# Attention layer of a four-layer graph kernel: scores from split halves, the mask on GpSimd, the normalisation shared with ScalarE

## The chip, the cores and the metric

The kernel runs on one core of a Trainium2 chip. The time is the device time of one execution, in microseconds (us). Five engines work side by side, each through its own queue in order: TensorE (PE in the profile), VectorE (DVE), ScalarE (ACT), GpSimd (POOL), and SyncE (SP), which here only starts transfers. They meet at semaphores: an instruction waits until a counter has reached a value. GpSimd works on SBUF alone; the other three reach PSUM too, into which TensorE writes.

## What is computed

Input `x` has 64 batches of 256 nodes with 128 features, `adj` is a 256x256 mask of zeros and ones. Four layers follow one another, each of the form `x = layernorm(x + layer(x))`. The change is in layer 0, the attention:

```python
def _L0_gnn_ref(x, A_shape, q, k, v):
    Q = x @ q
    K = x @ k
    A = jnp.einsum('bnd,bmd->bnm', Q, K)
    A = A / jnp.sqrt(jnp.float32(input_dimension))
    A = jnp.tanh(A / 8.0) * 8.0
    A = jnp.exp(A) * A_shape
    A = A / jnp.sum(A, axis=-1, keepdims=True)
    out = A @ x @ v
    return out

x = _layernorm(x + _L0_gnn_ref(x, adj, L0_gnn_q, L0_gnn_k, L0_gnn_v), axis=-1)
```

Layer 1 is five steps of a gated recurrence over `adj`, layer 2 a graph convolution up to the third power of `adj`, layer 3 a message layer. They are not touched.

## The kernel before

**Tiling.** Two batches make a group of 512 nodes, four tiles of 128 nodes; there are 32 groups. All five engines run the attention in slots, one group entering in each slot: `s` is the slot, and a step with a lag of L works in slot s on group s - L. The slots 0 to 7 and the last ones are written out, those between are a loop of four slots. Nothing schedules this: the order in which an engine's `slot` function names its steps is the order of its queue. In the profile's lines the functions `tensor`, `scalar`, `vector` and `gpsimd` of `attention_layer` are at L331 to L407, L410 to L438, L440 to L499 and L280 to L330.

**One group's way.** TensorE transposes `x` (L355) into a PSUM bank, ScalarE copies it to `x_t` (L417). TensorE forms the qk product `p` of it (L374; `qk` is q times k transposed, made once) and `x v` (L380), which ScalarE copies to `p_t` (L431) and `xv` (L434). A slot later TensorE forms the scores (L365), and ScalarE takes their tanh (L422) and exp (L426). VectorE multiplies by the mask (L449, 128x1024 numbers), TensorE sums over the nodes (L346; a column of ones in `xv` gives the denominator), VectorE takes the reciprocal (L454), scales and adds `x` (L457), takes the statistics (L462, `BN_STATS` in the order, `BATCH_NORM_STATS2` in the profile), combines them with six small instructions of 4 to 12 columns (L132 to L140, `combine_stats`), GpSimd raises the variance to the power -1/2 (L329, `ALU.pow`), and VectorE normalises (L475). SyncE stores the result.

**Types.** The matrix products of the attention are plain float32. The later layers split each operand instead into a `_hi` part of type float32r and a `_lo` part, the rest of it, and make three float32r products: hi by hi, lo by hi, hi by lo. The split takes a cast (ScalarE or GpSimd) and a subtraction (VectorE or GpSimd).

**What sets the order around the change.** TensorE's slot is: sum over the nodes of group s-3, transposes of s, scores of s-1, qk product and `x v` of s. ScalarE's is: `x_t` of s, tanh and exp of s-1, `p_t` and `xv` of s. VectorE's is: mask of s-2; reciprocal, scaling and statistics of s-3; normalisation of s-4; combining of s-3. GpSimd has one power a slot; before its first slot it prepares the weights of the later layers. `weave` lets the slots of the gated layer (layer 1) begin inside the last slots of the attention, at the numbers given to it, on each engine by itself:

```python
both = weave(attention["gpsimd"](pool), gated["gpsimd"](pool), [30, 31, 32, 33])
both = weave(attention["tensor"](pe), gated["tensor"](pe), [31, 32, 33, 34])
both = weave(attention["vector"](dve), gated["vector"](dve), [31.5, 32.5, 33.5, 34.5])
```

In those slots the gated layer's steps stand between the attention's: transposes L651, products with `adj` L663 and L665, gate products L676 to L708 on TensorE, `hn_lo` L758, `m_lo` L767 and `rh` L773 on VectorE, `rh_lo` L626, `h_hi` L630 and `h_lo` L632 on GpSimd.

Of the kernel before, what the change touches and what calls it, by code (L numbers as in the profile page):

```python
# [35 lines left out]
def adj_resnorm_d4_kernel(nc, t, out):  # L36
# [14 lines left out]
    with ExitStack() as top:  # L51
# [33 lines left out]
        with ExitStack() as ctx_gated:  # L85
# [4 lines left out]
            with ExitStack() as ctx_conv:  # L90
# [35 lines left out]
def combine_stats(dve, stats, moments, parts, var_eps, parts_done, terms_done, var_done, n):  # L126
# [11 lines left out]
    dve.tensor_scalar(moments[:, :, 1], moments[:, :, 1], 0.5, None, ALU.mult).then_inc(terms_done, 1)  # L138
# [4 lines left out]
def attention_layer(nc, t, psum, env, ctx):  # L143

    KC, N, D, GB, TILES, COLS, GROUPS = (env[k] for k in ("KC", "N", "D", "GB", "TILES", "COLS", "GROUPS"))
    x1_dram, ident, adj_t, qk, v, x_view, SCORE = (
        env[k] for k in ("x1_dram", "ident", "adj_t", "qk", "v", "x_view", "SCORE"))
# [6 lines left out]
    LAG_S, LAG_MASK, LAG_OUT, LAG_NORM, LAG_STORE = 1, 2, 3, 4, 5  # L154
# [5 lines left out]
    def sem(name):  # L160
# [4 lines left out]
    p_t = sb("p_t", [128, 2, COLS])  # L165
# [3 lines left out]
    y = sb("y", [128, 2, TILES, D])  # L169
# [32 lines left out]
    xt_done, pt_done, xv_done, cap_done, exp_done = (  # L202
        sem(n) for n in ("xt_done", "pt_done", "xv_done", "cap_done", "exp_done"))
# [13 lines left out]
    def run(eng, slot, lags, weights=None, behind=0, second=None):  # L217

        for it in range(PEELED):
            for u in range(U):  # L220
                slot(it, u)
                if second is not None:
                    second(it, u)
                if weights is not None and (it, u) == (0, 1):
                    weights()
        with eng.Fori(PEELED, GROUPS // U - 1) as it:
            for u in range(U):
                slot(it, u)
                if second is not None:
                    second(it, u)  # L230
        for s in range(GROUPS - U, GROUPS + lags):
            slot(s // U, s % U)
            if second is not None:
                yield s + behind - 0.5
                second(s // U, s % U)
            yield s + behind
# [5 lines left out]
    def sync(sp):  # L242
        def slot(it, u):
# [4 lines left out]
            if live(it, u, LAG_STORE):  # L248
                n, q = s - LAG_STORE, (u - LAG_STORE) % 2
                sp.wait_ge(x1_done, n + 1)  # L250
                sp.dma_start(x1_dram[bass.ds(n, 1), :, :].rearrange("o p c -> (o p) c"),
                             x1[:, q, :, :].rearrange("p i d -> p (i d)")).then_inc(x1_out[q], 16)
# [27 lines left out]
    def gpsimd(pool):  # L280
# [9 lines left out]
        pool.wait_ge(w_loaded, 16 * 10)  # L290
        for i, src in enumerate((1, 2, 0)):
            op = pool.tensor_tensor(w_sum[:, i, :], w_in[:, src, 0:D], w_in[:, src, D:2 * D], ALU.add)
        op.then_inc(w_summed, 1)
        pool.wait_ge(w_summed, 1)
        pool.tensor_tensor(w_dif[:, :], w_sum[:, 2, :], w_sum[:, 0, :], ALU.subtract).then_inc(w_ready, 1)
        pool.tensor_tensor(bias_cols[:, 6:8], bias_cols[:, 0:2], bias_cols[:, 3:4].broadcast_to([128, 2]), ALU.add)
        pool.tensor_tensor(bias_cols[:, 8:9], bias_cols[:, 2:3], bias_cols[:, 4:5], ALU.add)
        pool.wait_ge(adj_loaded, 16)
        pool.tensor_tensor(adj_sq_hi[:, :, :], adj_n[:, :, :], adj_n[:, :, :], ALU.mult)
        pool.wait_ge(conv_loaded, 16)  # L300
        by_power = conv_in[:, :].rearrange("p (o k) -> p k o", k=7)
        pool.tensor_copy(wcat[:, 3, :], by_power[:, 0, :])
        for j in range(1, 4):
            op = pool.tensor_tensor(wcat[:, 3 - j, :], by_power[:, j, :], by_power[:, j + 3, :], ALU.add)
        op.then_inc(wcat_done, 1)
        pool.wait_ge(wcat_done, 1)
        pool.tensor_copy(wc_hi[:, :, :], wcat[:, :, :]).then_inc(wc_hi_done, 1)
        pool.wait_ge(phi1m_loaded, 32)
        pool.tensor_copy(phi1m_hi[:, :], phi1m[:, :]).then_inc(wc_hi_done, 1)
        pool.tensor_copy(phi1x_hi[:, :], phi1x[:, :]).then_inc(wc_hi_done, 1)  # L310
        pool.wait_ge(rows_loaded, 32)
        pool.tensor_copy(row_hi[:, :, :], row_in[:, :, :]).then_inc(row_hi_done, 1)
        pool.wait_ge(wc_hi_done, 3)
        pool.tensor_tensor(wc_lo[:, :, :], wcat[:, :, :], wc_hi[:, :, :].bitcast(F32), ALU.subtract)
        pool.tensor_tensor(phi1m_lo[:, :], phi1m[:, :], phi1m_hi[:, :].bitcast(F32), ALU.subtract)
        pool.tensor_tensor(phi1x_lo[:, :], phi1x[:, :], phi1x_hi[:, :].bitcast(F32), ALU.subtract)
# [13 lines left out]
        yield from run(pool, slot, 0, behind=LAG_OUT)  # L330

    def tensor(pe):
        def slot(it, u):
            s = it * U + u
            if live(it, u, LAG_OUT):
# [14 lines left out]
            if live(it, u, 0):  # L350

                pe.wait_ge(x_loaded[u], (it + 1) * 16)
                wait_count(pe, xt_done, s)
                for i in range(TILES):
                    mm = pe.transpose(psum[:, B_XT, i * 128:(i + 1) * 128], x_in[:, u, i, :], ident[:, :])  # L355
                mm.then_inc(xt_mm, 1)
            if live(it, u, LAG_S):

                n, q = s - LAG_S, (u - LAG_S) % 2
                pe.wait_ge(pt_done, n + 1)  # L360
                wait_count(pe, cap_done, n)
                for b in range(GB):
                    for k in range(KC):
                        i = b * KC + k
                        mm = pe.matmul(psum[:, B_S + b, k * N:(k + 1) * N], x_t[:, q, i * 128:(i + 1) * 128],  # L365
                                       p_t[:, q, b * N:(b + 1) * N], start=True, stop=True)
                mm.then_inc(s_mm, 1)
            if live(it, u, 0):

                pe.wait_ge(xt_done, s + 1)  # L370
                wait_count(pe, pt_done, s)
                if isinstance(it, int) and s == 0:
                    pe.wait_ge(qk_done, 1)
                pe.matmul(psum[:, B_P, :], qk[:, :], x_t[:, u % 2, :], start=True, stop=True).then_inc(p_mm, 1)  # L374

# [7 lines left out]
        def weights():  # L383

            pe.wait_ge(w_ready, 1)
# [24 lines left out]
    def scalar(act):  # L410
        def slot(it, u):
            s = it * U + u
            if live(it, u, 0):
                act.wait_ge(xt_mm, s + 1)
                wait_count(act, s_mm, s - 1)
                wait_count(act, xv_mm, s - 1)
                act.copy(x_t[:, u % 2, :], psum[:, B_XT, :]).then_inc(xt_done, 1)  # L417
            if live(it, u, LAG_S):
                n, r = s - LAG_S, (u - LAG_S) % U
# [4 lines left out]
                act.wait_ge(cap_done, n + 1)  # L424
                wait_count(act, o_mm, n - U + 1)
                act.activation(e[:, r, :, :].rearrange("p i n -> p (i n)"), cap[:, :], ACT.Exp,  # L426
                               scale=8.0).then_inc(exp_done, 1)
            if live(it, u, 0):
                act.wait_ge(p_mm, s + 1)
                wait_count(act, s_mm, s - 1)  # L430
                act.copy(p_t[:, u % 2, :], psum[:, B_P, :]).then_inc(pt_done, 1)  # L431
# [6 lines left out]
        yield from run(act, slot, LAG_S)  # L438

    def vector(dve):  # L440
        def slot(it, u):
            s = it * U + u
            if live(it, u, LAG_MASK):

                n, r = s - LAG_MASK, (u - LAG_MASK) % U
                dve.wait_ge(exp_done, n + 1)
                eb = e[:, r, :, :].rearrange("p (b k) n -> p b (k n)", b=GB)
                mask = adj_t[:, :, :].rearrange("p (o k) n -> p o (k n)", o=1).broadcast_to([128, GB, KC * N])
                dve.tensor_tensor(eb, eb, mask, ALU.mult).then_inc(e_done, 1)  # L449
            if live(it, u, LAG_OUT):  # L450
                n, r, q = s - LAG_OUT, (u - LAG_OUT) % U, (u - LAG_OUT) % 2
                dve.wait_ge(o_mm, n + 1)
                sums = psum[:, B_O:B_O + GB, :].rearrange("p b (c n) -> p (b c) n", c=KC)
                dve.reciprocal(den[:, q, :], sums[:, :, D]).then_inc(den_done, 1)  # L454
                dve.wait_ge(den_done, n + 1)
                for i in range(TILES):
                    op = dve.scalar_tensor_tensor(out=y[:, q, i, :], in0=sums[:, i, 0:D], scalar=den[:, q, i:i + 1],  # L457
                                                  in1=x_in[:, r, i, :], op0=ALU.mult, op1=ALU.add)
                op.then_inc(y_done, 1)
                dve.wait_ge(y_done, n + 1)  # L460
                for i in range(TILES):
                    op = dve.bn_stats(stats[:, q, i, :], y[:, q, i, :])  # L462
                op.then_inc(stats_done, 1)

        def normalise(it, u):
            s = it * U + u
            if live(it, u, LAG_NORM):
# [6 lines left out]
                for i in range(TILES):  # L474
                    op = dve.tensor_scalar(x1[:, q, i, :], y[:, q, i, :], mv[:, q, i, 1:2], rstd[:, q, i:i + 1],  # L475
# [790 lines left out]
```

## Time and profile before

| | before |
|---|---|
| median of 3 runs (lowest, highest) | 1387.78 us (1387.11, 1387.89) |
| the profiled execution: time, span | 1387.39 us, 1385.2 us |
| busy share of the span: PE, PEld, DVE, ACT, POOL | 97%, 85%, 80%, 67%, 54% |
| chain that ended last, share by engine | PE 94%, DVE 3%, ACT 2%, issue 1% |
| attention, slots 0 to 31 | from about 7 to 183.7 us |
| mean granted TensorE clock | 0.992 |

The span is that of the profiled execution, from its first to its last instruction; the execution's own time is 2.2 us longer. The shares are means over all four layers; the change touches the first 190 us or so. There DVE is busy 53.4 of 60 us, ACT 37.5 and POOL 10.1, while PE is always busy (the stretch from 100 to 160 us).

### The profile page before, as it was taken

Reading aid. Unit: us, or ns where it says so; the run is one execution under the profiler, and the core shown is the slowest. Engines: PE = TensorE matmul, PEld = TensorE weight load, DVE = VectorE, ACT = ScalarE, POOL = GpSimd, SP = SyncE. Lnnn points to the kernel's source line nnn. Section 1 sums busy time; section 2 is a strip of 40 time slices with the busy share of each in tenths; the row PEclk is TensorE's granted clock in tenths of the full one; section 3 lists DMA queues with packets and bytes.
Section 4 is the critical chain, followed back from the end, with each engine's and each line's share of the span. In section 5 each row is a group of like instructions: output and inputs, shape, how many; then the busy total and the mean of one; then the engine's idle time right before and its main releaser. Section 6 shows DMA issues by size and latency. Waiting matters only on the chain.

```text
span 1385.2 us, 26908 instructions
## 1 busy us (share of the span) xinstructions
PE 1349.8 (97%) x8470; PEld 1184.3 (85%) x8470; DVE 1108.6 (80%) x2632; ACT 927.9 (67%) x1666; POOL 753.7 (54%) x745
## 2 busy tenths in 40 slices
PE   9999979999999999999999999999889999999995
PEld 7888868888888888888888888887689999999994
DVE  5888878777778777778777787777688888888885
ACT  5666647677777776777777777766546666666664
POOL 4111127666666666666666666665435555555553
PEclk9999999999999999999999999999999999999998
DMA  3222232000021000020000110000212222222211
GB/s 107 96 92 91 96 103 77 1 0 0 9 82 32 0 0 0 30 83 8 0 0 0 46 46 1 0 0 8 76 54 70 70 68 68 68 68 68 68 39 38
DMA packets 60041, 61.16 MB, mean 44 GB/s; under 512 B 4691, under 2 KB 39381, under 8 KB 59989
## 3 DMA queue, kind: packets, MB, share of 16 engines
q1 hardware_dynamic: 59556, 60.31, 13.6%
q8 instruction: 27, 0.44, 0.1%
q10 hardware_dynamic: 432, 0.20, 0.1%
q14 instruction: 26, 0.21, 0.0%
HBM read 35.33 MB, written 25.17 MB: 44 GB/s over the span
## 4 chain that ended last, share of the span: by engine, by line
PE 94%; DVE 3%; ACT 2%; issue 1%; POOL 0%; ACTq 0%; POOLq 0%; DVEq 0%
PE psum L969 6%; PE psum L663 5%; PE psum L665 5%; PE psum L651 5%; PE psum L346 4%; PE psum L365 4%; PE psum L981 3%; PE psum L983 3%; PE psum L706 3%; PE psum L695 3%; PE psum L678 3%; PE psum L707 3%; PE psum L676 3%; PE psum L696 3%; PE psum L699 3%; PE psum L698 3%
## 5 line engine op out<-in xcount | busy, mean ns | idle before, releaser
L626 POOL TENSOR_TENSOR rh_lo<-rh,rh_hi 128x512 fp32r<-128x512 f32 x160 | 207.1, 1294 | 265.6 <-ACT rh_hi L741 265.6
L632 POOL TENSOR_TENSOR h_lo<-h,h_hi 128x512 fp32r<-128x512 f32 x160 | 216.6, 1354 | 12.8
L741 ACT CAST rh_hi<-rh 128x512 fp32r<-128x512 f32 x160 | 99.4, 621 | 149.2 <-DVE rh L773 149.2
L754 DVE TENSOR_TENSOR psum<-psum,h 128x512 f32<-128x512 f32 x160 | 111.9, 699 | 103.5 <-ACT psum L745 103.5
L663 PE MATMUL psum<-adj_t_hi,hn_hi 128*128 128x256 f32 x640 | 172.1, 303 | 1.0 <-DVE m_lo L767 1.0
L738 ACT ACTIVATE psum<-psum,bias_cols 128x512 f32<-128x512 f32 x160 | 106.8, 667 | 80.1 <-PE psum L683 80.0
L665 PE MATMUL psum<-adj_t_hi,hn_lo 128*128 128x256 f32 x640 | 158.9, 282 | 0.0
L773 DVE TENSOR_TENSOR rh<-psum,h 128x512 f32<-128x512 f32 x160 | 110.1, 688 | 50.3 <-ACT psum L738 50.2
L663 PEld LDWEIGHTS psum<-adj_t_hi,hn_hi 128*128 128x128 f32 x640 | 121.8, 190 | 1.9 <-issue 1.8
L665 PEld LDWEIGHTS psum<-adj_t_hi,hn_lo 128*128 128x128 f32 x640 | 122.2, 191 | 0.0
L728 ACT ACTIVATE z<-psum,bias_cols 128x512 f32<-128x512 f32 x160 | 111.3, 695 | 0.0
L764 DVE TENSOR_TENSOR psum<-psum,z 128x512 f32<-128x512 f32 x160 | 110.3, 690 | 0.1
L329 POOL TENSOR_TENSOR rstd<-var_eps,minus_half 128x4 f32<-128x4 f32 x32 | 33.5, 1048 | 139.4 <-DVE var_eps L140 139.4
L777 DVE TENSOR_TENSOR h<-psum,h 128x512 f32<-128x512 f32 x160 | 108.8, 680 | 0.1
L767 DVE TENSOR_TENSOR m_lo<-psum,m_hi 128x512 fp32r<-128x512 f32 x160 | 108.8, 680 | 0.0
L1094 ACT CAST c_hi<-psum 128x512 fp32r<-128x512 f32 x96 | 56.3, 586 | 75.9 <-PE psum L983 47.0
L745 ACT ACTIVATE psum<-psum,bias_cols 128x512 f32<-128x512 f32 x160 | 104.6, 654 | 3.1 <-PE psum L700 3.1
L981 PE MATMUL psum<-c_hi,adj_t_hi 128*128 128x256 f32 x384 | 98.4, 291 | 5.5 <-DVE c_lo L1159 5.3
L630 POOL CAST h_hi<-h 128x512 fp32r<-128x512 f32 x160 | 98.0, 612 | 1.2 <-ACT hn_hi L722 1.2
L733 ACT CAST m_hi<-psum 128x512 fp32r<-128x512 f32 x160 | 94.6, 591 | 0.4 <-PE psum L665 0.4
L983 PE MATMUL psum<-c_lo,adj_t_hi 128*128 128x256 f32 x384 | 93.5, 278 | 0.0
L1159 DVE TENSOR_TENSOR c_lo<-psum,c_hi 128x512 fp32r<-128x512 f32 x96 | 65.5, 682 | 28.6 <-ACT c_hi L1094 28.0
(184 smaller groups left out, 4119.8 us busy)
## 6 DMA issues: line engine op xcount, KB each, us to landing
x_in<-in_x_dram SPq DMA_DIRECT2D x32, 256.0 KB, 2.8
x_dram<-x SPq DMA_DIRECT2D x32, 256.0 KB, 2.1
g_x<-x_dram SPq DMA_DIRECT2D x32, 256.0 KB, 3.3
h_dram<-h SPq DMA_DIRECT2D x32, 256.0 KB, 2.0
ht<-h_dram SPq DMA_DIRECT2D x32, 256.0 KB, 2.9
c_x<-x_dram SPq DMA_DIRECT2D x32, 256.0 KB, 3.1
out_dram<-res SPq DMA_DIRECT2D x32, 256.0 KB, 2.4
conv_in<-in_L_gnn_weight_dram SPq DMA_DIRECT2D x1, 448.0 KB, 4.8
```

The lines of the kernel that those rows point to most:

```text
L626: pool.tensor_tensor(rh_lo[:, q, :], rh[:, q, :], rh_hi[:, q, :].bitcast(F32), ALU.subtract).then_inc(rh_lo_done, 1)
L632: pool.tensor_tensor(h_lo[:, q, :], h[:, (g - 1) % G, :], h_hi[:, q, :].bitcast(F32), ALU.subtract).then_inc(h_lo_done, 1)
L663: pe.matmul(psum[:, B_M, b * N:(b + 1) * N], hn_hi[:, p, i, :], adj_hi[:, c, :], start=(c == 0), stop=False)
L665: mm = pe.matmul(psum[:, B_M, b * N:(b + 1) * N], hn_lo[:, p, i, :], adj_hi[:, c, :], start=False, stop=(c == KC - 1))
L728: act.activation(z[:, (g - 3) % 2, :], psum[:, B_GATE + (g - 3) % 2, :], ACT.Sigmoid, bias=B_Z).then_inc(z_done, 1)
L754: dve.tensor_tensor(cb, cb, hg, ALU.subtract).then_inc(dif_done, 1)
L764: dve.tensor_tensor(cb, cb, z[:, (g - 4) % 2, :], ALU.mult).then_inc(inc_done, 1)
L767: dve.tensor_tensor(m_lo[:, (g - 1) % 4, :], psum[:, B_M, :], m_hi[:, (g - 1) % 4, :].bitcast(F32), ALU.subtract).then_inc(m_lo_done, 1)
L773: dve.tensor_tensor(rh[:, q, :], psum[:, B_R, :], h[:, (g - 2) % G, :], ALU.mult).then_inc(rh_done, 1)
L777: dve.tensor_tensor(hg, cb, hg, ALU.add).then_inc(h_done, 1)
L981: pe.matmul(dst, lhs, flat(c_hi[:, level, k * GB:(k + 1) * GB, :]), start=False, stop=False, skip_group_check=True)
L983: mm = pe.matmul(dst, lhs, flat(c_lo[:, level, k * GB:(k + 1) * GB, :]), start=False, stop=(k == KC - 1), skip_group_check=True)
```

## The change

On TensorE the float32 scores and the qk product become three float32r products each, of halves `xt_hi`, `xt_lo`, `p_hi`, `p_lo`, `qk_hi`, `qk_lo`. The transposes move ahead of the sum over the nodes, and the qk product behind `x v`. For the halves ScalarE writes `p_hi` where it wrote `p_t`, GpSimd casts `x_t` to `xt_hi`, and VectorE makes `xt_lo` and `p_lo` (both read one operand from PSUM and one from SBUF). The mask moves from VectorE to GpSimd. Half of the normalisation's four tiles goes to ScalarE, as scale times `y` plus a `shift` that GpSimd multiplies. Combining and power come a slot later (lag 4), normalisation and store too (lags 5 and 6). GpSimd's preparation of weights is spread over its first seven slots, and VectorE's split of the gate weights comes behind its slot 1. The diff, cut to its core:

```diff
-                    both = weave(attention["gpsimd"](pool), gated["gpsimd"](pool), [30, 31, 32, 33])
+                    both = weave(attention["gpsimd"](pool), gated["gpsimd"](pool), [31, 32, 33, 34])
...
-    LAG_S, LAG_MASK, LAG_OUT, LAG_NORM, LAG_STORE = 1, 2, 3, 4, 5
+    LAG_S, LAG_MASK, LAG_OUT, LAG_COMBINE, LAG_NORM, LAG_STORE = 1, 2, 3, 4, 5, 6
...
         def slot(it, u):
-            n, q = it * U + u, u % 2
-
-            pool.wait_ge(var_done, n + 1)
-            pool.tensor_tensor(rstd[:, q, :], var_eps[:, q, :], minus_half[:, :], ALU.pow).then_inc(rstd_done, 1)
+            s = it * U + u
+            if live(it, u, 0):
+                pool.wait_ge(xt_done, s + 1)
+                wait_count(pool, s_mm, s - 1)
+            if live(it, u, LAG_NORM):
+                n, q = s - LAG_NORM, (u - LAG_NORM) % 2
+                pool.wait_ge(rstd_done, n + 1)
+                wait_count(pool, x1_half_done, n - 1)
+                pool.tensor_tensor(shift[:, q, :], mv[:, q, :, 1], rstd[:, q, :], ALU.mult).then_inc(shift_done, 1)
+            if live(it, u, 0):
+                pool.tensor_copy(xt_hi[:, u % 2, :], x_t[:, u % 2, :]).then_inc(xt_hi_done, 1)
+            if live(it, u, LAG_MASK):
...
+                pool.wait_ge(exp_done, n + 1)
...
+                pool.tensor_tensor(eb, eb, mask, ALU.mult).then_inc(e_done, 1)
+            if live(it, u, LAG_COMBINE):
+                n, q = s - LAG_COMBINE, (u - LAG_COMBINE) % 2
+                pool.wait_ge(var_done, n + 1)
...
+                pool.tensor_tensor(rstd[:, q, :], var_eps[:, q, :], minus_half[:, :], ALU.pow).then_inc(rstd_done, 1)
...
-                        mm = pe.matmul(psum[:, B_S + b, k * N:(k + 1) * N], x_t[:, q, i * 128:(i + 1) * 128],
-                                       p_t[:, q, b * N:(b + 1) * N], start=True, stop=True)
...
+                        pe.matmul(dst, xt_hi[:, q, tile], p_hi[:, q, cols], start=True, stop=False)
+                        pe.matmul(dst, xt_lo[:, q, tile], p_hi[:, q, cols], start=False, stop=False)
+                        mm = pe.matmul(dst, xt_hi[:, q, tile], p_lo[:, q, cols], start=False, stop=True)
...
-                pe.matmul(psum[:, B_P, :], qk[:, :], x_t[:, u % 2, :], start=True, stop=True).then_inc(p_mm, 1)
...
+                pe.wait_ge(xt_lo_done, s + 1)
...
+                pe.matmul(psum[:, B_P, :], qk_hi[:, :], xt_hi[:, u % 2, :], start=True, stop=False)
+                pe.matmul(psum[:, B_P, :], qk_lo[:, :], xt_hi[:, u % 2, :], start=False, stop=False)
+                pe.matmul(psum[:, B_P, :], qk_hi[:, :], xt_lo[:, u % 2, :], start=False, stop=True).then_inc(p_mm, 1)
```

VectorE's queue in one slot in the middle of the attention, before (mask, reciprocal, scaling, statistics, normalisation, combining):

```order
L449 TENSOR_TENSOR e<-e,adj_t 128x1024
L454 RECIPROCAL den<-psum 128x4
L457 SCALAR_TENSOR_TENSOR y<-psum,den,x_in 128x128 x4
L462 BN_STATS stats<-y 128x6 x4
L475 TENSOR_SCALAR x<-y,mv,rstd 128x128 x4
L132 TENSOR_TENSOR mv<-stats 128x12
L133 TENSOR_TENSOR parts<-stats 128x4
L135 TENSOR_SCALAR parts<-mv 128x4
L136 SCALAR_TENSOR_TENSOR parts<-parts 128x4
L138 TENSOR_SCALAR mv<-mv 128x4
L140 TENSOR_TENSOR var_eps<-parts 128x4
```

VectorE's queue in the same slot, changed (L508 is `p_lo` of group s-1, L531 `xt_lo` of group s):

```order
L508 TENSOR_TENSOR p_lo<-psum,p_hi 128x512
L132 TENSOR_TENSOR mv<-stats 128x12
L133 TENSOR_TENSOR parts<-stats 128x4
L135 TENSOR_SCALAR parts<-mv 128x4
L136 SCALAR_TENSOR_TENSOR parts<-parts 128x4
L138 TENSOR_SCALAR mv<-mv 128x4
L140 TENSOR_TENSOR var_eps<-parts 128x4
L522 RECIPROCAL den<-psum 128x4
L525 SCALAR_TENSOR_TENSOR y<-psum,den,x_in 128x128 x4
L531 TENSOR_TENSOR xt_lo<-psum,xt_hi 128x512
L536 BN_STATS stats<-y 128x6 x4
L549 TENSOR_SCALAR x<-y,mv,rstd 128x128 x2
```

The mask has left this queue. The six combining instructions have moved from the slot's end to its head, behind `p_lo` and ahead of the reciprocal, and `xt_lo`, on which the qk product waits, stands behind all of them.

GpSimd's queue in that slot, changed; before it held one row, the power (L329 then):

```order
L351 TENSOR_TENSOR shift<-mv,rstd 128x4
L353 CAST xt_hi<-x_t 128x512
L362 TENSOR_TENSOR e<-e,adj_t 128x1024
L368 TENSOR_TENSOR rstd<-var_eps,minus_half 128x4
L351 TENSOR_TENSOR shift<-mv,rstd 128x4
```

The last row is the next slot's first. The cast and the mask stand ahead of the power, and the first three start when ScalarE's `x_t` of this slot is done.

ScalarE's queue in that slot, before and then changed (L464 is `p_hi`, L483 the half of the normalisation):

```order
L417 COPY x_t<-psum 128x512
L422 ACTIVATE cap<-psum 128x1024
L426 ACTIVATE e<-cap 128x1024
L431 COPY p_t<-psum 128x512
L434 COPY xv<-psum 128x4x128
```

```order
L464 CAST p_hi<-psum 128x512
L468 COPY x_t<-psum 128x512
L473 ACTIVATE e<-cap 128x1024
L483 ACTIVATE x<-y,shift,rstd 128x128 x2
L490 ACTIVATE cap<-psum 128x1024
L495 COPY xv<-psum 128x4x128
```

The exp of a group has moved a slot behind its tanh, to the place right behind `x_t`, so it now starts early in the slot.

## Rows read from the trace of the kernel before

**Rows 1.** Chain of work, one attention slot: start us, us, engine, output, line, instructions.
```profile
105.82 0.44 PE psum L355 x4
106.26 1.73 PE psum L365 x8
107.99 0.86 PE psum L374 x2
108.85 0.89 PE psum L380 x8
109.74 1.79 PE psum L346 x16
```

**Rows 2.** Chain of work in the gated layer, float32r products of 256 and 512 columns.
```profile
503.09 0.12 PE psum L665
...
504.15 0.23 PE psum L677
```

**Rows 3.** Timeline of ScalarE in that slot: start us, us, engine, line, op [idle <-releaser].
```profile
108.03 1.02 ACT L422 ACTIVATE cap<-psum 128x1024 f32<-128x1024 f32 x1 [1.14 <-PE psum L365]
109.08 1.06 ACT L426 ACTIVATE e<-cap 128x1024 f32<-128x1024 f32 x1
110.04 0.57 ACT L431 COPY p_t<-psum 128x512 f32<-128x512 f32 x1
110.51 0.59 ACT L434 COPY xv<-psum 128x512 f32<-128x512 f32 x1
```

**Rows 4.** Timeline of VectorE, a slot later: combining, reciprocal, scaling.
```profile
114.75 0.17 DVE L132 TENSOR_TENSOR mv<-stats 128x12 f32<-128x12 f32 x1
...
115.37 0.16 DVE L140 TENSOR_TENSOR var_eps<-parts 128x4 f32<-128x4 f32 x1
...
117.27 0.18 DVE L454 RECIPROCAL den<-psum 128x4 f32<-128x4 f32 x1 [0.17 <-PE psum L346]
117.48 1.13 DVE L457 SCALAR_TENSOR_TENSOR y<-psum,den,x_in 128x128 f32<-128x128 f32 x4
```

**Rows 5.** Timeline of GpSimd where the attention ends beside the gated layer.
```profile
208.60 1.35 POOL L626 TENSOR_TENSOR rh_lo<-rh,rh_hi 128x512 fp32r<-128x512 f32 x1 [9.83 <-ACT rh_hi L741]
209.89 0.61 POOL L630 CAST h_hi<-h 128x512 fp32r<-128x512 f32 x1
210.58 1.30 POOL L632 TENSOR_TENSOR h_lo<-h,h_hi 128x512 fp32r<-128x512 f32 x1
```

**Rows 6.** Timeline of VectorE in the same stretch, the last group's combining.
```profile
208.72 1.26 DVE L132 TENSOR_TENSOR mv<-stats 128x12 f32<-128x12 f32 x1
209.90 0.62 DVE L133 TENSOR_TENSOR parts<-stats 128x4 f32<-128x4 f32 x1
...
210.63 1.27 DVE L136 SCALAR_TENSOR_TENSOR parts<-parts 128x4 f32<-128x4 f32 x1
...
212.10 0.69 DVE L758 TENSOR_TENSOR hn_lo<-g_x,hn_hi 128x512 fp32r<-128x512 f32 x1
```

**Rows 7.** Timeline of VectorE and GpSimd 16 us earlier.
```profile
192.72 1.13 DVE L457 SCALAR_TENSOR_TENSOR y<-psum,den,x_in 128x128 f32<-128x128 f32 x4
...
193.36 1.26 POOL L632 TENSOR_TENSOR h_lo<-h,h_hi 128x512 fp32r<-128x512 f32 x1
```

**Rows 8.** Timeline of GpSimd at the start, a product of 128 columns.
```profile
11.00 0.46 POOL L295 TENSOR_TENSOR w_dif<-w_sum 128x128 f32<-128x128 f32 x1
```

**Rows 9.** Timeline of ScalarE in the last layer, normalisation with scale and shift.
```profile
1213.31 1.64 ACT L1118 ACTIVATE res<-y,c_shift,c_rstd 128x128 f32<-128x128 f32 x4
```

**Rows 10.** Timeline of VectorE at the start, first and last of four splits.
```profile
14.41 0.42 DVE L492 CAST ug_hi<-psum 128x256 fp32r<-128x256 f32 x1 [6.10 <-PE psum L389]
...
15.67 0.55 DVE L497 TENSOR_TENSOR wg_lo<-psum,wg_hi 128x384 fp32r<-128x384 f32 x1
```

**Rows 11.** Timeline of TensorE at the attention's end, third group of the gated layer.
```profile
195.49 0.63 PE L651 MATMUL psum<-ident,g_x 128*128 128x128 f32 x4 [3.03 <-DVE hn_lo L758]
```

**Rows 12.** Window: us, busy of PE, PEld, DVE, ACT, POOL, granted clock, DMA share, GB/s.
```profile
197.00:198.00 1.00, 1.00 (x6) 0.90 (x5) 0.61 (x6) 0.59 (x2) 0.25 (x1) 0.50 0.15 55
```

More of the change, by code:

```diff
@@ L164, in attention_layer @@
     x_t = sb("x_t", [128, 2, COLS])
-    p_t = sb("p_t", [128, 2, COLS])
+    xt_hi = sb("xt_hi", [128, 2, COLS], F32R)
+    xt_lo = sb("xt_lo", [128, 2, COLS], F32R)
+    p_hi = sb("p_hi", [128, 2, COLS], F32R)
+    p_lo = sb("p_lo", [128, 2, COLS], F32R)
+    qk_hi = sb("qk_hi", [128, D], F32R)
+    qk_lo = sb("qk_lo", [128, D], F32R)
+    shift = sb("shift", [128, 2, TILES])
+    HALF = TILES // 2
     xv = sb("xv", [128, U, TILES, 132])
@@ L215, in attention_layer, with run @@
     B_QKT, B_QK, B_ADJ, B_U, B_W = 4, 5, 6, 7, 2
[L217 to L225, printed above, removed]
+    def run(eng, slot, lags, between=None, second=None):
+        for s in range(PEELED * U):
+            slot(s // U, s % U)
+            if second is not None:
+                second(s // U, s % U)
+            if between is not None:
+                between(s)
         with eng.Fori(PEELED, GROUPS // U - 1) as it:
@@ L297, in gpsimd @@
[L297 to L304, printed above, removed]
@@ L332, in tensor @@
+        yield from run(pool, slot, LAG_NORM, prepare)
     def tensor(pe):
@@ L334, in slot @@
             s = it * U + u
+            if live(it, u, 0):
+                pe.wait_ge(x_loaded[u], (it + 1) * 16)
+                wait_count(pe, xt_lo_done, s)
+                for i in range(TILES):
+                    mm = pe.transpose(psum[:, B_XT, i * 128:(i + 1) * 128], x_in[:, u, i, :], ident[:, :])
+                mm.then_inc(xt_mm, 1)
             if live(it, u, LAG_OUT):
@@ L412, in slot @@
             s = it * U + u
+            if live(it, u, LAG_S):
+                n, q = s - LAG_S, (u - LAG_S) % 2
+                act.wait_ge(p_mm, n + 1)
+                wait_count(act, s_mm, n - 1)
+                act.copy(p_hi[:, q, :], psum[:, B_P, :]).then_inc(p_hi_done, 1)
             if live(it, u, 0):
                 act.wait_ge(xt_mm, s + 1)
-                wait_count(act, s_mm, s - 1)
                 wait_count(act, xv_mm, s - 1)
                 act.copy(x_t[:, u % 2, :], psum[:, B_XT, :]).then_inc(xt_done, 1)
+            if live(it, u, LAG_MASK):
+                n, r = s - LAG_MASK, (u - LAG_MASK) % U
+                act.wait_ge(cap_done, n + 1)
+                wait_count(act, o_mm, n - U + 1)
+                act.activation(e[:, r, :, :].rearrange("p i n -> p (i n)"), cap[:, :], ACT.Exp,
+                               scale=8.0).then_inc(exp_done, 1)
+            if live(it, u, LAG_NORM):
+                n, q = s - LAG_NORM, (u - LAG_NORM) % 2
+                act.wait_ge(shift_done, n + 1)
+                if not isinstance(it, int):
+                    act.wait_ge(x1_out[q], it * (16 * U // 2) + 16 * ((u - LAG_NORM) // 2))
+                elif n >= 2:
+                    act.wait_ge(x1_out[q], 16 * (n // 2))
+                for i in range(HALF, TILES):
+                    op = act.activation(x1[:, q, i, :], y[:, (u - LAG_NORM) % U, i, :], ACT.Identity,
+                                        bias=shift[:, q, i:i + 1], scale=rstd[:, q, i:i + 1])
+                op.then_inc(x1_half_done, 1)
             if live(it, u, LAG_S):
-                n, r = s - LAG_S, (u - LAG_S) % U
+                n = s - LAG_S
                 act.wait_ge(s_mm, n + 1)
@@ L437, in scalar @@
         act.dma_start(v[:, :], t["L0_gnn_v"]).then_inc(v_loaded, 16)
-        yield from run(act, slot, LAG_S)
+        yield from run(act, slot, LAG_NORM)
     def vector(dve):
@@ L442, in slot @@
             s = it * U + u
[L443 to L449, printed above, removed]
+            if live(it, u, LAG_S):
+                n, q = s - LAG_S, (u - LAG_S) % 2
+                dve.wait_ge(p_hi_done, n + 1)
+                wait_count(dve, s_mm, n - 1)
+                dve.tensor_tensor(p_lo[:, q, :], psum[:, B_P, :], p_hi[:, q, :].bitcast(F32),
+                                  ALU.subtract).then_inc(p_lo_done, 1)
+            if live(it, u, LAG_COMBINE):
+                n, q = s - LAG_COMBINE, (u - LAG_COMBINE) % 2
+                dve.wait_ge(stats_done, n + 1)
+                wait_count(dve, shift_done, n - 1)
+                wait_count(dve, x1_done, n - 1)
+                combine_stats(dve, stats[:, q, :, :], mv[:, q, :, :], parts[:, q, :, :], var_eps[:, q, :],
+                              parts_done, mv_done, var_done, n)
             if live(it, u, LAG_OUT):
```

167 lines of the change are left out of this document (94 added, 73 removed).

## Prediction

> **What bounds the kernel now.** I read the chain of work first. In the middle of the attention it holds nothing but TensorE, five groups of products back to back: 0.44 us of transposes, 1.73 of scores, 0.86 of the qk product, 0.89 of x v and 1.79 of the sum over the nodes, 5.71 us a slot [rows 1]. Then the timelines of the other engines, for what each has to spare in such a slot. VectorE starts the reciprocal 0.17 us after its own last work was done, when TensorE's sum ends [rows 4], so it is nearly as full as TensorE; ScalarE waits 1.14 us for the scores [rows 3]; GpSimd has one power a slot. So TensorE sets the time, with VectorE close behind. Last I looked for what an instruction of VectorE does when GpSimd works beside it, since the change gives GpSimd a long one. From the slot's length, slot 3 ends at 109.74 - 15 x 5.705 = 24.2 us and slot 31 at 183.7.
>
> **What the halves save.** A float32r product takes 0.12 us for 256 columns with weights of its own, and 0.23 for 512 [rows 2]. The scores become 12 x 0.118 = 1.42 us instead of 1.73, the qk product 3 x 0.232 = 0.70 instead of 0.86 (the 0.118 and 0.232 are means over a slot's run of such pieces; the rows are rounded). That is 0.47 us a slot, 15.0 us over 32 slots, and TensorE's own slot becomes 5.24 us. It is a gain only where nothing else ends later.
>
> **The chain that takes TensorE's place.** In the new order the qk product of s waits for `xt_lo` of s, and VectorE makes that behind combining, reciprocal and scaling. I follow one slot from T = 0, the end of the qk product of s-1.
> - ScalarE starts `p_hi` 0.04 us later (as tanh follows the scores: 106.26 + 1.73 = 107.99, start 108.03 [rows 1, 3]). Copies follow each other by 0.47 us (110.04 to 110.51), so `x_t` runs from 0.51 to 1.10. The exp of s-2 has its tanh from the slot before; it starts at 0.98 and, 1.06 long, ends at 2.04 [rows 3].
> - GpSimd waits for `x_t`. A step behind a semaphore comes 0.08 us later (209.89 + 0.61 = 210.50, then 210.58 [rows 5]): `shift` at about 1.18. A product of 128 columns takes 0.46 and one of 512 takes 1.30 [rows 5, 8], so 0.0022 us a column on a fixed 0.18. `shift` (4 columns) takes 0.2, `xt_hi` 0.61 until about 1.97, and the mask (1024 columns) 0.18 + 1024 x 0.0022 = 2.42; the bounds are 2.3 and 2.6 (twice 1.30). It waits for the exp, so it runs from 2.12 to 4.54.
> - VectorE makes `p_lo` at 0.66 (0.69 us long [rows 6], its successor 0.1 earlier than its end) and combines from 1.26 on. Unhindered that is 0.70 us (114.75 to 115.37 and a last 0.08 [rows 4]), to 1.96, ahead of the sum's end at 0.44 + 1.79 = 2.23, and costs nothing.
>
> But it is not unhindered. Where GpSimd's long instructions stood beside the combining of the last group, L132, L133 and L136, 0.17 us long elsewhere, took 1.26, 0.62 and 1.27, and ended at 209.98, 210.52 and 211.90, each 0.02 or 0.03 after GpSimd's running instruction (209.95, 210.50, 211.88) [rows 5, 6]. What these three read lies in SBUF with both operands; `y`, which reads PSUM and SBUF, ran its usual 1.13 beside `h_lo` [rows 7]. L140 is of the first kind too. So four of six combining instructions cannot run beside GpSimd's, and the cast counts like the product.
>
> Combining starts at 1.26, `xt_hi` runs until 1.97: one of L133 and L136 is held to there. After a held L133, L136 comes 0.11 us later (210.52, 210.63); after a held L136, L140 about 0.12 later (the next instruction but one starts at 212.10, 0.20 after 211.90 [rows 6]). Either comes at about 2.10, and the mask at 2.12 at the latest. If L136 wins that, L140 follows at 2.3 and is held all the same. So one of them waits until 4.56. The reciprocal then starts between 4.48 (L140 held) and 4.76 (L136 held), `y` 0.21 later (117.27 to 117.48 [rows 4]), `xt_lo` another 1.05, ends 0.69 after that, at 6.43 to 6.71; TensorE needs 0.05 to start, 0.70 for the product and 0.1 for a cold start of its queue. The slot is 7.3 to 7.55 us; I take 7.45. In the next slot everything stands to its T as in this one, so the hold repeats. TensorE is through with x v at 4.54 and idles for 2.2 us.
>
> The Trainium skill has a rule on this pair, "SBUF — State Buffer", section Who interferes with whom: an instruction of VectorE with two SBUF inputs and one of GpSimd that reads SBUF exclude each other, and the later one waits for the whole of the earlier. The three rows agree, but none is longer than 1.35 us. By the rule the 2.4 us of the mask count in full; were a hold never longer than the rows', the slot would be about 1.1 us shorter.
>
> What else moves, and why it costs nothing in such a slot: ScalarE's two normalising instructions, 0.41 each (a quarter of 1.64 [rows 9]), fit between the exp and the scores at 3.65; GpSimd's power starts behind the mask; VectorE, with statistics and half of the normalisation after `xt_lo`, is done before the next `p_lo`; stores have a slot more.
>
> **The sum**, against the profiled execution's 1387.4 us (median 1387.8, so no correction):
> - Slots 0 to 3, which have no combining: -1.9 from the halves. The chain `x_t`, `xt_hi`, `xt_lo` outlasts x v in slot 0 by 0.5. In slot 1 `p_hi` and `p_lo` (0.04 + 0.59 + 0.69) have only 0.44 us of transposes as cover: 1.0. In slot 2 `p_lo` stands behind the four splits of the gate weights, 14.41 to 16.22 [rows 10]: 2.0 of idle TensorE. Together +1.6.
> - 28 slots, 4 to 31, of 7.45 instead of 5.71: +48.7. Bounds: 7.3 and 7.55 give +44.5 and +51.5.
> - The end of the attention. TensorE already waits there for `hn_lo`, 3.03 us for the third gated group [rows 11], and it stands behind combining and `y`. Two masks fall into these slots, each with up to 2.4 us of hold: +5, bounds 0 and +10. GpSimd's weight preparation finds room beside slots of 7.4 us: 0.
>
> 1387.4 + 1.6 + 48.7 + 5 = 1442.7, so **1443**, own range 1425 to 1455.
>
> **Rivals.**
> - *The clock falls in the gaps.* The granted clock was 0.50, the 1.2 GHz level, from 197 us on [rows 12], after an idle of 3.03 us [rows 11]; whether 2.2 us in every slot would do the same, no row shows. At the low level the qk product takes 0.7 more and `x_t` comes 0.4 later: 1.1 us a slot. In half of 28 slots that is +15: 1458.
> - *No hold, or a harmless one (faster).* It needs the last combining instruction to begin before the mask. That is the case if the mask comes later than I have it, by 0.2 us or more: if the exp, or GpSimd's start behind it, is late. For it: the race is within a tenth or two of a microsecond. Against it: combining cannot start before 1.26 and meets `xt_hi` anyway. Then `xt_lo` is ready at about 4.2, before TensorE wants it at 4.54, and TensorE's 5.24 rule: 1387.4 - 15.0 + 3.5 + 3 = 1379.
> - *The race goes either way from slot to slot.* Half the slots at 7.45, half at 5.24: 28 x (0.5 x 1.74 - 0.5 x 0.47) = +18, with 1.6 and 4 about 1411.
>
> **Chances.** Forecast 0.61, clock 0.17, no hold 0.14, mixed 0.08. The range reaches down to the mixed case and up to the clock's: 1410 to 1465; it leaves out the faster case. Within 0.2% (2.8 us, about what a measurement of this kernel can tell from no change) only the edges of two cases fall: 0.02. Faster 0.14, slower 0.84.
>
> **What the changed profile would show.** Right: one of L136 and L140 with a mean far over 0.17 us, towards 2.4 if it is L136, ending with GpSimd's mask (L362) in every slot; TensorE's L424 waiting about 2.2 us in each for `xt_lo` (L531); 7.3 to 7.55 us from slot to slot in the chain, with VectorE in it; pieces of 0.12 for the scores. Wrong: combining of 0.7 us and a chain of TensorE alone (the faster case); a mask much longer or shorter than 2.4 us; a granted clock under 1.0 between 30 and 230 us (the clock's case).

## The result, and the profile after

| | before | changed |
|---|---|---|
| median (lowest, highest) | 1387.44 us (1385.87, 1387.89) | 1429.34 us (1426.19, 1432.35) |
| ratio to before, 95% interval | | 1.0304 (1.0276 to 1.0332) |
| the profiled execution: time, span | 1387.39, 1385.2 us | 1432.35, 1430.6 us |

The change costs 42 us, 3%. The forecast said slower, and its range holds the time; but the mechanism that it named is not the one that works in the changed kernel. Of all executions reported here one, of the kernel before with the transposes moved and eight buffers for `x`, took 3243.76 us; it counts in its median of ten and not in its ratio.

The page of the changed kernel, span, busy shares and the chain's shares by engine:

```profile
span 1430.6 us, 27674 instructions
...
PE 1346.6 (94%) x8630; PEld 1189.0 (83%) x8630; DVE 1096.1 (77%) x2601; ACT 953.7 (67%) x1730; POOL 853.2 (60%) x841
...
PE 84%; DVE 6%; DMA 6%; ACT 2%; issue 2%; POOL 0%; SPq 0%; ACTq 0%; DVEq 0%; POOLq 0%
```

The new thing is DMA, 6% of a chain that had none before. Where it sits shows in the chain of work in the middle of the attention (start us, us, what):

```profile
102.48 2.94 DMA x_in<-in_x_dram
...
105.46 0.66 PE psum L379 x4
106.12 1.80 PE psum L392 x16
...
107.94 0.19 DVE den L522
...
108.43 0.87 DVE y L525 x3
...
109.47 2.63 DMA x_in<-in_x_dram
...
112.22 0.65 PE psum L379 x4
```

Read it as a ring: load of `x`, transposes (L379), sum over the nodes (L392), reciprocal, `y`, and the next load, 6.76 us here and 6.84 on average over slots 4 to 31, against 5.71 in [rows 1]. The link that closes it is a buffer. `x_in` has four of them, and SyncE may load group s only when `y` of group s-4, the last reader of that buffer, is done. That `y` is made in slot s-1, behind that slot's sum. With the transposes ahead of the sum, each slot's sum waits for its transposes, and these for a load that waited for the sum of the slot before. TensorE's waits from 20 to 220 us (us in all, times, longest) hold nothing else worth a line:

```profile
PE psum L379 <- DMA x_in<-in_x_dram: 38.2, 28, 1.6
```

And combining is not held. Timelines of VectorE, GpSimd and TensorE in that slot:

```profile
105.19 0.16 DVE L132 TENSOR_TENSOR mv<-stats 128x12 f32<-128x12 f32 x1
...
105.82 0.16 DVE L140 TENSOR_TENSOR var_eps<-parts 128x4 f32<-128x4 f32 x1
107.94 0.18 DVE L522 RECIPROCAL den<-psum 128x4 f32<-128x4 f32 x1 [1.96 <-PE psum L392]
...
109.20 0.68 DVE L531 TENSOR_TENSOR xt_lo<-psum,xt_hi 128x512 fp32r<-128x512 f32 x1
```
```profile
106.95 0.61 POOL L353 CAST xt_hi<-x_t 128x512 fp32r<-128x512 f32 x1
107.78 2.40 POOL L362 TENSOR_TENSOR e<-e,adj_t 128x1024 f32<-128x1024 f32 x1 [0.21 <-ACT e L473]
```
```profile
109.98 0.48 PE L424 MATMUL psum<-xt_hi,qk_hi 128*128 128x512 f32 x1
```

Combining (105.19 to 105.98) has ended 0.97 us before GpSimd starts its cast. `x_t` comes late, because the transposes do, so GpSimd's work has slipped past the combining; VectorE then idles 1.96 us for the sum (in [rows 4] 0.17), and `xt_lo` is there at 109.88, before TensorE wants it at 109.98. L136 and L140 have means of 156 and 163 ns over 20 slots, as in the kernel before.

### The profile page after: what moved, and what is told of

It is laid out like the page before. It is cut to its first block, busy times and chain, and to the rows that moved or that the text cites. A ratio compares the mean times of both kernels' runs of the same rounds, so it can differ in the third digit from the quotient of the medians.

```text
span 1430.6 us, 27674 instructions
## 1 busy us (share of the span) xinstructions
PE 1346.6 (94%) x8630; PEld 1189.0 (83%) x8630; DVE 1096.1 (77%) x2601; ACT 953.7 (67%) x1730; POOL 853.2 (60%) x841
## 4 chain that ended last, share of the span: by engine, by line
PE 84%; DVE 6%; DMA 6%; ACT 2%; issue 2%; POOL 0%; SPq 0%; ACTq 0%; DVEq 0%; POOLq 0%
PE psum L1046 6%; DMA x_in<-in_x_dram 5%; PE psum L740 5%; PE psum L742 5%; PE psum L728 5%; PE psum L392 4%; PE psum L1058 3%; PE psum L1060 3%; PE psum L783 3%; PE psum L784 2%; PE psum L785 2%; PE psum L755 2%; PE psum L772 2%; PE psum L753 2%; PE psum L773 2%; PE psum L776 2%
## 5 line engine op out<-in xcount | busy, mean ns | idle before, releaser
L1022 POOL TENSOR_TENSOR x3b<-x,phi_b 128x512 f32<-128x512 f32 x32 | 41.1, 1284 | 82.3 <-ACT x3t L1179 79.4
L1031 POOL TENSOR_TENSOR c_rstd<-c_var_eps,c_minus_half 128x4 f32<-128x4 f32 x32 | 32.6, 1020 | 94.5 <-DVE c_var_eps L1287 94.5
```

## Where the 45 us between the two spans came from

- *Slots 0 to 3, +4.6.* They end at about 28.8 us instead of 24.2. In slot 2 the scores wait 2.07 us behind the four splits, and after that TensorE's granted clock is 0.57 for 4 us, about 1.7 us lost. The line is of TensorE's timeline, the second of the windows (columns as in [rows 12]):

```profile
18.87 0.39 PE L406 MATMUL psum<-p_hi,xt_hi 128*128 128x256 f32 x1 [2.07 <-DVE p_lo L508]
```
```profile
20.00:24.00 4.00, 4.00 (x20) 3.69 (x19) 0.00 (x0) 1.84 (x3) 2.86 (x5) 0.57 0.01 4
```

- *28 slots of the ring, +31.7.* They run from 28.8 to 220.2 us, 6.84 a slot: 28 x 1.13.
- *The end, +7.9.* From the transposes of the first gated group to those of the sixth are 42.9 us, before 35.0. TensorE's three waits for `hn_lo` take 11.1 us there, 7.4 before. Here the hold does act, once. Timelines of GpSimd, VectorE and TensorE, and the window:

```profile
223.48 2.38 POOL L362 TENSOR_TENSOR e<-e,adj_t 128x1024 f32<-128x1024 f32 x1 [2.54 <-ACT e L473]
```
```profile
223.51 2.38 DVE L138 TENSOR_SCALAR mv<-mv 128x4 f32<-128x4 f32 x1
```
```profile
229.78 1.09 PE L728 MATMUL psum<-ident,g_x 128*128 128x128 f32 x4 [4.86 <-DVE hn_lo L835]
```
```profile
224.00:260.00 36.00, 23.39 (x122) 19.71 (x121) 23.20 (x67) 15.33 (x28) 19.10 (x20) 0.86 0.07 24
```

That is 44.2 of 45.4 us.

## The experiments

Theories: **ring**, the load waits for `y` of four groups before; **hold**, the prediction's own, one combining instruction waits for GpSimd's mask, and `xt_lo` behind it. Where expectations use letters, A is the ring, B the hold, C a second ring that the transposes' old place would close, through `x_t` and GpSimd's mask, and D says that the end costs what the place of `hn_lo` in VectorE's queue makes it cost.

**The move of the transposes alone, in the kernel before.** The edit, in `tensor`:

```diff
+            if live(it, u, 0):
+                pe.wait_ge(x_loaded[u], (it + 1) * 16)
+                wait_count(pe, xt_done, s)
+                ...  (the four transposes)
             if live(it, u, LAG_OUT):   # the sum over the nodes
...
-            if live(it, u, 0):
-                pe.wait_ge(x_loaded[u], (it + 1) * 16)
...
```

> The kernel before with one move of the change alone: TensorE's four transposes of a slot stand ahead of the sum over the nodes. Nothing else is changed, nothing is left out. Theory A (the load ring): the load of x for slot s waits for the scaling y of group s-4, which VectorE makes in slot s-1 behind the sum of that slot; with the transposes ahead of the sum, load, transposes, sum, reciprocal, y form a ring of 2.8 + 0.66 + 1.80 + 0.2 + 1.2 and some 0.2 of hand-overs = 6.85 us, as in the changed kernel. Expected: about 6.85 us a slot on 27 or 28 slots instead of 5.71, so some 31 us slower, 1417 to 1421 us, with TensorE waiting 1.1 to 1.5 us a slot for the load. Theory B (the hold of the combining by GpSimd's mask, as predicted): there is no mask on GpSimd here, so nothing changes, 1386 to 1390 us.

Measured: 1416.43 us, ratio 1.0213 (1.0196 to 1.023). No float32r, no mask on GpSimd, no new lag, and 30 us are gone. Its waits, TensorE, 20 to 230 us:

```profile
PE psum L340 <- DMA x_in<-in_x_dram: 24.0, 28, 1.6
```

With the longer start after each of the 28 waits (0.22 us, see the last section) the 24.0 us make 30.

**The same with eight buffers for `x`.** The loop becomes one of eight slots; the rings of `e` and `xv` stay four long:

```diff
-    U = 4
+    U = 8
+    R = 4
...
-    PEELED = 2
+    PEELED = 1
...
-    xv = sb("xv", [128, U, TILES, 132])
+    xv = sb("xv", [128, R, TILES, 132])
...
-    e = sb("e", [128, U, TILES, N])
+    e = sb("e", [128, R, TILES, N])
```

> The kernel before with the four transposes ahead of the sum and eight buffers for x, nothing else. Load ring (theory): the whole +30 us of the move came from the load of x waiting for y of four groups before; with eight buffers the load has four slots more, TensorE's slot is 5.7 us again, no wait of the transposes for a load: 1384 to 1390. Rival, the move costs by itself (a later reciprocal and y, x_t too early for ScalarE's order): stays at 1405 to 1420.

Measured: 1385.24 us, ratio 0.9994 (0.9984 to 1.0003). All 30 us are back. Its chain is TensorE alone again, with slots of 5.70 us; the two transposes that follow each other:

```profile
104.44 0.44 PE psum L341 x4
...
110.14 0.44 PE psum L341 x4
```

So the move costs nothing by itself; it costs because of the buffers. This pair settles the cause for the kernel before; for the changed kernel the next four do.

**The changed kernel, transposes back behind the sum.**

```diff
-            if live(it, u, 0):
-                pe.wait_ge(x_loaded[u], (it + 1) * 16)
...
             if live(it, u, LAG_OUT):   # the sum over the nodes
...
+            if live(it, u, 0):
+                pe.wait_ge(x_loaded[u], (it + 1) * 16)
```

> The changed kernel with the transposes back behind the sum over the nodes, where they were before; the rest of the change stays. Theory A: the load is off the ring. If nothing takes its place, TensorE's own 5.24 us a slot rule and the time is 1429 - 28 x 1.6 = 1384 us. Rival C: a second ring closes, since ScalarE's exp stands behind x_t, and x_t now comes 1.8 us later: sum 1.80, transposes 0.44, x_t 0.47, exp 1.06, mask 2.40, hand-overs 0.2 = 6.3 to 6.4 us from one sum to the next, which needs that mask. Then 1429 - 28 x 0.5 = 1413 to 1416 us, with TensorE waiting for GpSimd's mask ahead of the sum. Theory B would have the combining held: it does not meet the mask here, so B expects 1384 too.

Measured: 1422.78 us, ratio 1.0264 (1.0246 to 1.0281). The load is out of the way, and a second ring has taken its place. TensorE's waits from 60 to 200 us, then the chain:

```profile
PE psum L385 <- POOL e L362: 18.4, 22, 1.0
```
```profile
107.24 2.05 PE psum L385 x16
109.29 0.45 PE psum L394 x4
...
109.84 0.60 ACT x_t L468
...
110.73 0.20 POOL shift L351
110.93 0.53 POOL xt_hi L353
...
111.46 2.38 POOL e L362
...
113.89 0.38 PE psum L385
```

Sum, transposes, `x_t`, GpSimd's two small steps, mask, and the next sum waits for the mask: 6.65 us (6.57 to 6.67 in slots 4 to 30). The rival on record had this ring, 0.3 us too short: it left `shift` and the cast out (0.73 us ahead of the mask) and took 1.80 for a sum that, after a wait, lasts 2.05. So neither place of the transposes is good with this GpSimd queue and four buffers: ahead of the sum they break the second ring and close the first.

**The changed kernel with eight buffers** (same edit as above, with `y` four long too).

> The changed kernel with eight buffers of x instead of four (loops of eight slots for it), so that a load waits for the scaling of group s-8 and not s-4. Nothing else is moved. Theory A: the load is off the ring, and TensorE's wait for it goes to 0. Then it is seen what is next. With B in force (x_t now starts 0.5 us after the qk product, GpSimd's cast and mask start early, and the combining is held until the mask's end) a slot is 7.3 to 7.55 us and the time 1441 to 1450 us, slower than the changed kernel, with L136, L138 or L140 over 2 us long. Without a hold the slot is 5.24 us and the time 1384 us.

Measured: 1444.15 us, ratio 1.0408 (1.0388 to 1.0429): with the load's wait gone the kernel is *slower*. What was hidden comes out. Timelines of GpSimd, VectorE and TensorE in one slot, and TensorE's waits from 20 to 240 us:

```profile
110.84 2.39 POOL L363 TENSOR_TENSOR e<-e,adj_t 128x1024 f32<-128x1024 f32 x1 [0.21 <-ACT e L474]
```
```profile
111.03 2.23 DVE L140 TENSOR_TENSOR var_eps<-parts 128x4 f32<-128x4 f32 x1
113.19 0.17 DVE L523 RECIPROCAL den<-psum 128x4 f32<-128x4 f32 x1
...
114.43 0.68 DVE L532 TENSOR_TENSOR xt_lo<-psum,xt_hi 128x512 fp32r<-128x512 f32 x1
```
```profile
115.17 0.50 PE L425 MATMUL psum<-xt_hi,qk_hi 128*128 128x512 f32 x1 [1.92 <-DVE xt_lo L532]
```
```profile
PE psum L425 <- DVE xt_lo L532: 40.0, 23, 2.2
```

L140, 0.16 us of work, ends at 113.26, and the mask at 113.23. TensorE's transposes come at 108.53 and 115.97, 7.44 us apart. Of the 27 such distances from slot 4 on, 17 are 7.41 to 7.46 us; their mean is 7.35. Over 60 to 200 us the groups of lines have L140 with a mean of 1854 ns:

```profile
L140 DVE TENSOR_TENSOR var_eps<-parts 128x4 f32<-128x4 f32 x19 | 35.2, 1854 | 0.6
```

The clock's rival appears too, and brings the mixed one with it. From 60 to 120 us the granted clock was 0.94 here, and 1.00 in the changed kernel. Four times a slot of 7.8 to 8.3 us, at whose end the clock falls (0.68 from 102 to 106 us), is followed by one of 6.2 to 6.5, in which the mask comes too late to hold combining (it starts at 104.80 in one of them, and L140 ends at 104.62). The window from 60 to 120 us:

```profile
60.00:120.00 60.00, 50.07 (x373) 47.29 (x373) 53.68 (x157) 36.34 (x60) 35.55 (x35) 0.94 0.24 75
```

**Eight buffers, and combining behind `xt_lo`.**

```diff
         def slot(it, u):      # vector
-            if live(it, u, LAG_COMBINE):   # behind p_lo
-                ...  combine_stats(...)
...
+            if live(it, u, LAG_COMBINE):   # behind xt_lo
+                ...  combine_stats(...)
```

> As the kernel with eight loads, and the six combining instructions of VectorE moved behind xt_lo, so that xt_lo no longer stands behind them. Theory B: what was lost in the kernel with eight loads is had back here, 5.24 to 5.4 us a slot, 1384 to 1389 us; the combining may still be held by the mask, but nothing of TensorE waits for it. If there was no hold in the kernel with eight loads, both have the same time.

Measured: 1389.04 us, ratio 1.0021 (1.0009 to 1.0033), 55 us less than without the move. The chain is TensorE alone, and the slot is 5.25 us, the halves' own (two of its transposes):

```profile
131.48 0.44 PE psum L380 x4
...
136.73 0.44 PE psum L380 x4
```

A combining instruction is still held in places (L132, mean 472 ns from 60 to 200 us), but nothing that TensorE wants stands behind it.

Eight buffers do not give the load four slots more, though. In SyncE's queue the load of a group stands behind the store of the group seven before it, and now waits there for the normalisation, `x` (waits of SyncE from 60 to 170 us; for `y` there is none), then its timeline:

```profile
SPq L260 <- DVE x L551: 75.8, 21, 3.7
```
```profile
132.87 0.36 SPq L260 DMA_DIRECT2D x_dram<-x  x1
133.44 0.38 SPq L255 DMA_DIRECT2D x_in<-in_x_dram  x1
```

The transposes of that group start 3.1 us behind this load (136.57), and a load takes 2.9 here to land: it is off the ring with 0.2 us to spare. In the kernel before with eight buffers that distance is 5.0 us (133.51 to 138.49).

**Combining behind `xt_lo` alone, with four buffers.**

> The changed kernel with the combining behind xt_lo and nothing else, four buffers as before. Load ring (theory): combining does not stand in the ring, so the slot stays at 6.8 to 6.9 us and the transposes wait for the load as before: 1425 to 1433. Rival, the hold of the combining bounds the changed kernel (the prediction's mechanism): the time falls to 1385 to 1395.

Measured: 1425.97 us, ratio 1.0288 (1.0271 to 1.0305). TensorE's waits, 20 to 230 us:

```profile
PE psum L379 <- DMA x_in<-in_x_dram: 37.9, 28, 1.5
```

The four variants make a square:

| | combining ahead of `y` | combining behind `xt_lo` |
|---|---|---|
| four buffers | 1429.34 (slot 6.84) | 1425.97 (6.83) |
| eight buffers | 1444.15 (7.44) | 1389.04 (5.25) |

The times come from three sessions, in which the kernel before took 1387.44, 1386.45 and 1385.89 us; the slots are means from slot 4 on, those of the lower row the most frequent ones (means 7.35 and 5.43). Either cause alone keeps the kernel slow; only with both gone is TensorE the bound. Judged by one edit in the changed kernel, the hold would be worth 3 us at most (the intervals of the two ratios overlap), and the ring less than nothing.

**Why 5.25 us a slot gives nothing.** 28 x 0.46 = 12.9 us would be won in the middle. They go again: slot 4 begins 3.8 us late, slots 6 to 8, beside GpSimd's weight preparation, take 2.8 more, the other middle slots 2.1 (1.1 of them slot 30, at whose end the transposes wait 0.99 us for a load of `x`), and the end takes 41.9 us against 35.0, since `hn_lo` stands behind VectorE's attention steps. Three edits test that: VectorE's gated slots come half a slot earlier; at the start the four splits go behind `p_lo` of slot 2, GpSimd's preparation of slots 2 to 4 comes a slot earlier and that of slots 5 and 6 waits until slots 24 to 26; and both. The first of them:

```diff
-                    both = weave(attention["vector"](dve), gated["vector"](dve), [31.5, 32.5, 33.5, 34.5])
+                    both = weave(attention["vector"](dve), gated["vector"](dve), [31, 32, 33, 34])
```

> The kernel with eight loads and late combining, and one number list changed: VectorE's steps of the gated layer begin after slot 31 and not in the middle of slot 32 (31, 32, 33, 34 instead of 31.5 to 34.5), so that hn_lo no longer stands behind reciprocal, y and statistics of the same slot. At the attention's end TensorE waits 10.3 us for hn_lo there, and the clock falls to 0.5 twice. Theory D (the end costs what hn_lo's place in VectorE's queue makes it cost): most of these 10 us go, less what VectorE then waits itself; 1389 - 8 = 1381 us, between 1377 and 1385. Rival: VectorE stands at hn_lo waiting for ScalarE instead and y slips by as much, 1387 to 1391 us.

> The kernel with eight loads and late combining, with two moves at the start: VectorE's four splits of the gate weights stand behind p_lo of slot 2 and not ahead of it, and GpSimd's preparation of weights is moved off slots 4 to 6 (to slots 1 to 3 and 24 to 26). In the kernel it starts from, slot 4 begins at 27.96 us (some 3.8 behind the kernel before), of which 1.9 are the splits, and slots 6 to 8 take 5.96, 6.02 and 6.55 us instead of 5.25. Theory: 1.9 and 2.8 us are had back, 1384 us. Rival: the preparation only moves to where it delays xt_hi of slots 1 to 3, 1387 to 1389 us.

> Both of the above in one kernel. If the two stretches are independent, the gains add: 1389 - 8 - 4.7 = 1376 us. The halves' own gain of 15 us then is nearly all there, less 3 to 4 us of start.

Measured: 1379.28 us (0.9955, 0.9941 to 0.9968), 1384.64 (0.9983, 0.9974 to 0.9992) and 1377.62 (0.9931, 0.9917 to 0.9944). TensorE's wait for `hn_lo` without and then with the earlier weave, from 20 to 240 us:

```profile
PE psum L730 <- DVE hn_lo L837: 10.3, 3, 3.6
```
```profile
PE psum L730 <- DVE hn_lo L837: 0.4, 1, 0.4
```

The earlier weave is worth 9.8 us, the eased start 4.4, and both together 11.4, less than their sum. With the start eased slots 4 to 7 are 5.24 us each; slot 8 takes 7.1, behind a load of `x` that took 4.88 us, and slots 26 and 27, where the moved preparation now stands, 5.7 and 7.2. The last version is faster than both kernels, by 0.7% and 3.6%. But the weave is no part of the change, so it was put into the kernel before as well:

> The kernel before with the same change of VectorE's numbers alone (31 to 34 instead of 31.5 to 34.5). It tells how much of what the end costs has nothing to do with the change. TensorE waits there for hn_lo 1.3, 3.0 and 3.0 us and runs 6.8 us at clock 0.5. Theory D: 1386.5 - 6 = 1380 us. Rival: VectorE has the mask in its queue here as well, and y slips: 1385 to 1388 us.

Measured: 1380.78 us (0.9956, 0.9943 to 0.997). Two thirds of the 9 us are thus to be had without any halves. With its two stalls removed and the start eased, what the change adds beside the weave is 3.2 us (1380.78 to 1377.62), of the 12.9 that the middle could give.

## The prediction, step by step

- **Direction and size.** 1443 was forecast, 1429 measured, slower as said. That agreement is partly luck: another stall, which made a slot 1.13 us longer than before, stood where one that makes it 1.74 longer was forecast, and the ends cost 5.9 us more than in the sum. Of the four signs that the prediction named for being right, only the pieces of 0.12 us came. Whoever had mended the kernel by the prediction alone, moving the combining, would have won 3 us at most.
- **The halves: right.** Score pieces of 0.12 us, a slot of 5.25 where nothing stalls (forecast 5.24).
- **The mask: right.** 2.42 was worked out from products of 128 and 512 columns, 2.40 measured.
- **The step that failed** is the sentence that has `x_t` run from T + 0.51. T is the end of the qk product of s-1; `p_hi` starts 0.04 later, so in the slot shown T is 103.93, and `x_t` started at 106.15, T + 2.22. The transposes were taken as free to start at T. The working followed each engine's queue and left out the one queue that the move of the transposes touches first, SyncE's load, although what was needed lay in the trace of before. Its transfers of `x` (KB, median us to landing), SyncE's issue, and TensorE's transposes that use it:

```profile
x_in<-in_x_dram SPq DMA_DIRECT2D x5, 256.0 KB, 2.8
```
```profile
118.80 0.38 SPq L247 DMA_DIRECT2D x_in<-in_x_dram  x1
```
```profile
122.77 0.60 PE L355 MATMUL psum<-ident,x_in 128*128 128x128 f32 x4
```

  The load lands at 118.80 + 2.8 = 121.6, and the transposes come at 122.77: 1.2 us to spare, with a sum of 1.79 us ahead of them. Moved ahead of that sum they are 0.6 us short, and the ring closes. Its length from rows of before is 0.44 + 1.79 [rows 1], 0.21 + 1.13 for reciprocal and `y` [rows 4], 0.19 to the issue and 2.8 for the load: 6.56, plus 0.22 for transposes that start cold (0.66 here, 0.44 before), 6.8. Measured 6.84. The middle term would have been 28 x 1.09 = +30.5 in place of +48.7, and it was +31.7.
- **The hold: real, and in the wrong kernel.** With eight buffers the slot is the forecast one almost to the hundredth. With T = 108.69 the mask starts at T + 2.15 (forecast 2.12) and ends at 4.54 (4.54); L140 ends at 4.57 (4.56), `xt_lo` at 6.42 (6.43 where L140 is the one held); the slot is 7.44 (7.45). The changed kernel never gets there, since two stalls that lie side by side in a slot don't add up: the load's delay moves GpSimd's work behind the combining and so removes the hold. This was the condition of the rival *no hold*, "if the mask comes later than I have it"; it came true, but what made the mask late had a price of its own, which the rival left out.
- **The rule of the Trainium skill** ("SBUF — State Buffer", section Who interferes with whom), that the later of the two waits for the whole of the earlier, agrees: L140 waited 2.1 us, to the mask's end, though the mask had started only 0.2 us before it. L138 at the end of the attention did the same (2.2 us).
- **The start: the term mis-sized.** +1.6 was forecast, +4.6 measured. The wait behind the four splits was right (2.0 forecast, 2.07 measured); about 1.7 us of half clock behind it were not in the sum, and 0.7 are a later first transpose (7.34 us, before 6.62). The rest, under 1 us, is not taken apart.
- **The end: +5 forecast, +7.9 measured,** within its bounds of 0 and 10. The hold accounts for 2.2 us once; a granted clock of 0.86 over 36 us (0.91 before, from 188 to 224 us) is part of the rest, which no run takes apart for this kernel.
- **The rivals.** *No hold* is told above. The slots of the changed kernel did not go either way by turns, they were all near the ring's length (6.6 to 7.1); in the eight-buffer kernel four of 27 did, each time behind a fall of the clock. *The clock* did not apply to the changed kernel's middle (1.00 from 30 to 220 us with waits of 1.1 to 1.6 us in each slot); with waits of 1.9 to 2.2 us in most, in the eight-buffer kernel, the granted clock was 0.94. Its price, half the slots at 1.1 us, was too high there: the mean slot was 7.35, below the forecast one.

## To carry to other kernels

Whoever moves a step that reads a loaded buffer must ask when that load may start: write down the buffer count, who reads last, and how much the transfer had to spare, and compare that slack with the work that is jumped over (here 1.2 us against 1.79). Then close every ring through every queue, transfers included, before one of them is priced; the longest sets the slot, and the others stay hidden until it is gone. Count a queue's own order as a link too: a load can wait behind a store that it has nothing to do with. And when an experiment that removes a suspect changes nothing, or makes it worse, remove the two suspects together before either is dismissed.

## What the runs showed of the hardware beyond what was expected

- Float32 `TENSOR_SCALAR` instructions with a single tile as input are held by GpSimd as well; the prediction had counted only those that read two tiles from SBUF. L138, 128x4, took 2.38 us beside the mask (shown above, 223.51), and in the eight-buffer kernel, where in some slots it comes where L140 does in others:

```profile
118.43 2.36 DVE L138 TENSOR_SCALAR mv<-mv 128x4 f32<-128x4 f32 x1
```

  So in that chain it made no difference which of the combining instructions met the mask. The Trainium skill's page "SBUF — State Buffer" (Who interferes with whom) lists `tensor_scalar` among the operations that can take the shared ports; the row agrees.
- A run of float32 matmuls that starts after a wait is longer: four transposes 0.66 us in the chain instead of 0.44, a sum over the nodes 2.05 instead of 1.79 to 1.80. Most of it is the start of the first product, which otherwise lies beside the end of the product ahead (the transposes of 110.14 in the eight-buffer chain start at 109.98 in its timeline). In a ring this is paid in every turn.
